# Opening of an attention and expert kernel: two projections moved in among the first score maxima, a row load moved behind the first unit's loads, fewer filler products

## The reference, cut to what matters

```python
# x: (8, 256, 512)   ctx: (8, 256, 512)   mask: (8, 1, 512)
x = x + xattn(layernorm(x), ctx, mask, mask, Wq, bq, Wk, bk, Wv, bv)
x = x + ffn(layernorm(x), router, shared experts, 8 routed experts, top 2)

def xattn(target, source, target_mask, source_mask, ...):      # 16 heads of 16
    q = Wq @ target + bq;  k = Wk @ source + bk;  v = Wv @ source + bv
    dot = einsum('bhdt,bhds->bhts', q, k) / 4
    mask = target_mask[..., None] * source_mask[..., None, :]
    amap = softmax(mask * dot - (1 - mask) * 1e6) * mask
    return einsum('bhts,bhds->bhdt', amap, v)
```

## Time and profile before

| | |
|---|---|
| Time before, median of 3 runs | 689.02 us (688.03 to 693.57) |
| Span of the profiled execution, first to last instruction | 651.7 us |
| Own time of the profiled execution | not shown beside its span |
| Busy share: PE, DVE, ACT, POOL | 93%, 78%, 72%, 55% |
| Chain that ended last, by engine | PE 76%, DVE 11%, issue 6%, ACT 5% |
| Stretch that the change touches | about 21 to 60 us of the span |

### The profile page before, as it was taken

One profiled execution on the slowest core, in us unless ns is written; L12 is line 12 of the kernel. 1 busy time (PEld: TensorE's weight loads), 2 busy tenths in 40 slices (PEclk: granted clock), 3 DMA queues, 4 the chain that ended last, 5 costly groups with the idle time before them and its releaser, 6 DMA issues.

```text
span 651.7 us, 12576 instructions
## 1 busy us (share of the span) xinstructions
PE 606.6 (93%) x4110; PEld 259.2 (40%) x4110; DVE 507.6 (78%) x970; ACT 472.0 (72%) x662; POOL 360.0 (55%) x494
## 2 busy tenths in 40 slices
PE   4799999999999999999999999879999999999987
PEld 4543333333333333333333332224554466666532
DVE  2479899999999999999999999964528654454577
ACT  3654899899899899899898888985432276667511
POOL 5559453684684684684684462251553577777310
PEclk9899999999999999999999999999999999999999
DMA  8642434534525535534433432115698533333178
GB/s 293 195 135 76 114 93 145 168 110 144 170 87 168 167 89 171 167 112 146 135 111 102 132 111 80 50 52 121 170 220 184 110 105 106 100 106 107 50 230 310
DMA packets 64990, 88.66 MB, mean 136 GB/s; under 512 B 12624, under 2 KB 45264, under 8 KB 63904
## 3 DMA queue, kind: packets, MB, share of 16 engines
q1 hardware_dynamic: 60032, 68.72, 34.4%
q0 software_dynamic: 4896, 19.14, 12.1%
HBM read 63.75 MB, written 32.74 MB: 148 GB/s over the span
## 4 chain that ended last, share of the span: by engine, by line
PE 76%; DVE 11%; issue 6%; ACT 5%; DMA 1%; POOL 1%; SPq 0%; ACTq 0%; DVEq 0%; POOLq 0%
PE PS L1083 17%; PE PS L986 11%; PE PS L1311 9%; PE PS L1055 8%; PE PS L1774 7%; DVE MX L996 7%; PE PS L845 5%; PE PS L1837 4%; PE PS L1585 4%; ACT E L1069 2%; PE PS L840 2%; PE PS L991 1%; PE PS L933 1%; PE PS L1732 1%; PE PS L929 1%
## 5 line engine op out<-in xcount | busy, mean ns | idle before, releaser
L996 DVE TENSOR_REDUCE MX<-PS 128x1 f32<-128x512 f32 x512 | 323.1, 683 | 17.3 <-PE PS L986 15.4
L1069 ACT ACTIVATE E<-PS 128x1024 f32<-128x1024 f32 x256 | 253.5, 1020 | 32.7 <-PE PS L1055 28.6
L986 PE MATMUL PS<-BIG 53*128 53x512 f16 x512 | 128.6, 384 | 12.2 <-DVE MX L996 10.8
L1083 PE MATMUL PS<-E,BIG 128*32 128x512 f32 x1024 | 136.4, 605 | 2.0 <-ACT E L1069 2.0
L1055 PE MATMUL PS<-BIG 55*128 55x512 f16 x512 | 101.2, 381 | 8.2 <-ACT E L1069 3.5
L879 POOL TENSOR_TENSOR ML<-BIG,ML 128x512 f32<-128x512 f32 x30 | 38.3, 1277 | 102.8 <-ACT BIG L855 102.6
L986 PEld LDWEIGHTS PS<-BIG 53*128 53x128 f16 x512 | 34.3, 93 | 134.0 <-DVE MX L996 120.1
L1796 DVE SCALAR_TENSOR_TENSOR E<-WP,PS 128x352 bf16<-128x352 f32 x39 | 20.3, 521 | 47.0 <-ACT WP L1786 47.0
L1774 PE MATMUL PS<-BIG,CT 128*128 x312 | 53.0, 313 | 1.8 <-DVE WP L1346 1.0
L855 ACT ACTIVATE BIG<-PS,BIG 128x256 f32<-128x256 f32 x64 | 35.7, 560 | 25.9 <-PE PS L840 14.5
L1856 POOL DMA_INDIRECT scr_ys<-SW,bvB x39 | 38.3, 981 | 20.8 <-DVE SW L1849 12.5
(11 more groups left out here) (261 smaller groups left out, 904.0 us busy)
## 6 DMA issues: line engine op xcount, KB each, us to landing
scr_parts<-WP SPq DMA_DIRECT2D x96, 128.0 KB
BIG<-scr_parts SPq DMA_DIRECT2D x64, 192.0 KB
BIG<-in_we POOLq DMA_DIRECT2D x8, 1088.0 KB, 14.1
scr_u<-ML SPq DMA_DIRECT2D x32, 256.0 KB, 3.0
X<-in_x SPq DMA_DIRECT2D x8, 512.0 KB, 6.5
CT<-in_ctx SPq DMA_DIRECT2D x8, 512.0 KB, 4.1
ML<-scr_u SPq DMA_DIRECT2D x16, 256.0 KB
ML<-scr_recs SPq DMA_DIRECT2D x16, 256.0 KB
```

Of the source, the lines that this page charges most:

```text
L986: e.matmul(PS[:, yi[name] % 3, :], QK[rows, qb(u), 0, j0 + jj, 128 * tt:128 * tt + 128], QK[rows, qb(u), 1, j0 + jj, :], start=True, stop= ...
L996: e.tensor_reduce(MX[:, g % 2, c:c + 1], PS[:, yi[name] % 3, :], AX.X, ALU.max)\
L1069: e.activation(E[:, st, 2 * jj:2 * jj + 2, :], PS[:, slot(name):slot(name) + 2, :], ACT.Exp, scale=1 / 1024).then_inc(s["rc"], 1)
L1083: ins = e.matmul(PS[32 * hh:32 * hh + 32, AVB, :], VT[:, b % 2, st, 4 * (g % 4) + hh, :], E[:, st, hh, :], start=(st == 0), stop=(st == 3))
```

## The change

- `WARM` goes from (3, 1) to (1, 1): one filler product instead of three behind each score product of group 0.
- The two halves of k of unit 1 move from in front of the score products of group 0 to behind the fourth and the eighth of them. The two parts of v of unit 1 move from the same place to behind the tenth and the twelfth.
- With them move what is placed relative to them: the splitting of k on POOL, the writes of k, the scaling of v, and the load of source and mask of batch 2 on SP, which now stands behind the read-back of q of unit 1 instead of in front of it.
- The load of x of batch 2 moves on SP from in front of the writes of k of unit 0 to behind the read-backs of q and k of unit 0.
- ACT's scaling of the shared weights (`upper`) moves from -.95 to -.8, behind the two copies of k. POOL's `lower` moves from -.9 to -.7, behind the splitting of k, and so in front of the scaling of v of unit 1.
- The read-back of k of unit 1 moves a little later, to stand behind its writes.

```diff
-WARM = (3, 1)
+WARM = (1, 1)
...
         for w in range(NU):
+            tk = (-.93, -.82) if w == 1 else (w - 3 + 6.65 * IT, w - 3 + 7.85 * IT)
             ring += [(w - 3 + 3.75 * IT, ("q", w, 0)), (w - 3 + 4.75 * IT, ("q", w, 1)),
-                     (w - 3 + 6.65 * IT, ("k", w, 0)), (w - 3 + 7.85 * IT, ("k", w, 1))]
-            tv = -1 - .25 * IT if w == 1 else w - 2 + 0.65 * IT
+                     (tk[0], ("k", w, 0)), (tk[1], ("k", w, 1))]
+            tv = -.72 if w == 1 else w - 2 + 0.65 * IT
             mring += [(tv, ("v", w, 0)), (tv + (.1 if w == 1 else 1.0499999999999998) * IT, ("v", w, 1))]
...
         for b in range(2, B):
-            sp.at(2 * b - 6 + .02, load_x(b))
+            sp.at(-1.5 if b == 2 else 2 * b - 6 + .02, load_x(b))
...
-            act.at(-.95, upper)
+            act.at(-.8, upper)
...
-                pool.at(-.9, f)
+                pool.at(-.7, f)
...
-            sp.at(w - 2 + (2.9 if i else .9) * IT if w else -1.8 + .05 * i, emit)
+            sp.at(w - 2 + (3.6 if i and w == 1 else 2.9 if i else .9) * IT if w else -1.8 + .05 * i, emit)
```

## The result

The changed kernel takes 705.94 us (median of 5, 704.75 to 711.96) where the kernel before takes 689.02 (688.03 to 693.57): ratio 1.0257, 95% interval 1.0209 to 1.0304. It is 16.9 us slower; the forecast was 0.8 us faster. When it was measured again in another session (a session is one set of measurements, the kernel before among them) it took 673.94 beside 656.83, ratio 1.0262 (1.0226 to 1.0298), 17.1 us. The stage of the experts, which the change does not touch, took some 35 us more in the first two sessions than in the last two, for every kernel alike, so each kernel is compared only with the kernel before of its own session. Three executions of one experiment and five of another, whose mean clock was low, are left out of their ratios, but they are told of there, since whether the clock holds is the question.

What follows compares the result with a forecast made beforehand. It took PE's own work to bound 27.4 to 47 us. Terms: -3.2 (start of group 0) + 0.0 (group 0) + 2.3 (half clock) + 0.1 = -0.8, so 689.0 becomes 688.2 us; range 685.3 to 692.0.

Steps and rivals of the forecast that it cites:

- How long it lasts: PE from the start of group 0: half clock lasts 5.1 us, bounds 3.8 and 6.9.
- term of 2.3 us in the sum: PE in group 0: loss from half clock, 5.1 us at 0.455 us each, bounds 1.7 to 3.1.
- The first rival: PE from 28.7 us: half clock stays; 696.1 if through all of group 0, 690.9 if some 11 us; chance 0.16.
- The rival's price for group 0, 10.2 us: Group 0 wholly at half clock: 16 x 0.96 + 4 x 1.71 = 22.2 us, 10.2 more; a quarter of 0.16.
- What I held against it: Against lasting half clock: PE never idle (0.96 against DVE's 0.62), halves of k as dense as work that raised it.
- Fillers for real work, group 0 at 12.0 us at full clock: PE in group 0: 32 fillers (3.5 us) replaced by four projections (3.4 us), so it stays at 12.0 us.
- Start of group 0: First score product at 31.8 us instead of 35.03, after k's read-back: 3.2 us won, bounds 1.5 to 3.5.
- my signs of being wrong: First score product after 33.5, clock back after 39, PE waiting for `place` near 58 or 72, or group 2's shift lost.
- Row load: Load of x of batch 2 on SP: issued at about 30, 0.49 us, in front of nothing that is due.
- ACT, POOL and SP: Work moved off PE's path hides with 1 to 3 us to spare; 0.1 us charged, bounds 0 and 0.9.
- The 37.3 us between median and span: Whole kernel: the median is 37.3 us above the profiled span of 651.7, and the change has no hold on that.
- Everything behind group 1 shifts as a whole: From group 1 on, the order of work is the same and shifts as a whole, by -0.8 us in sum.

Runs made afterwards that it cites:

- the run with the gap closed: Changed kernel with 28 fillers ahead of the sum of squares of batch 1 and 56 ahead of the first score product: 655.03 us beside 656.98, ratio 0.9975.
- the run with the row load alone: Kernel before with only the load of x of batch 2 moved behind the read-backs of unit 0: 693.35 us, ratio 0.9989.
- the filled gap with 36 fillers: Changed kernel with 28 fillers ahead of the sum of squares, 36 ahead of the first score product: 692.49 us, ratio 0.9971 (eight of eleven executions).
- warm projections in front: Kernel before with the load of x of batch 2 moved and 28 fillers ahead of the sum of squares: 663.1 us, ratio 0.9999 (better five).
- the dense run: Changed kernel with 30 fillers ahead of the first score product, none ahead of the sum of squares: 656.16 us, ratio 1.0000.

## Why the prediction was wrong

The step that failed is "How long it lasts", 5.1 us with bounds of 3.8 and 6.9. It lasted 42 us, from 34.77 to about 77, and 48 us in the second profile of the changed kernel. The term of 2.3 us in the sum measured 17.5 over both groups. I took the length from rises behind unbroken projections and carried it over to a stream of score products with fillers. The first rival had the mechanism and its sign, and was given 0.16. What I held against it was that PE would never be idle at half clock. That was right (busy 2.00 of every 2.00 us) and worth nothing: here the busy share did not tell whether the clock would rise. I also held against it that the two halves of k are as dense as the work under which the clock rose before. Each is, but it lasts 1.7 us and stands between score products; of the runs that came to group 0 at half clock with one filler, only the one with all four projections in one block of 5.9 us (37.65 to 43.58) had a rise in group 0, 4.8 us into it. The rival's price for group 0, 10.2 us, measured 8.6 (20.53 less 11.96), since a score product at half clock takes 0.86 us, not 0.96 (doubling the streamed part alone, my 0.85, had been right); but I let it end with group 0, and group 1, with one filler as well, paid 8.9 more. I had read from group 1 of the kernel before that one filler is enough "once the clock is up". The run with the gap closed bears that out, where projections stand in between; that it is not enough to bring it up is another question, which the profile of before could not answer, since it shows no score product at half clock.

The Trainium skill's warnings pointed the right way. The Trainium skill (TensorE: Matmul & The Clock Gate, section "HAM oscillation — how this bites in real kernels") warns of idle gaps, after which work starts at half clock, and its section "A second HAM failure mode: psum-queue depth-cycling" warns of streams that idle briefly between groups. The trace agrees with the first (half clock behind 3.2 and 4.2 us idle). The second goes only part of the way: in the kernel before with one filler the clock fell in a filler at 39.57 before PE had idled at all in that group, and in the changed kernel it stayed at half with PE never idle.

Point by point:
- Fillers for real work, group 0 at 12.0 us at full clock: right. In the run with the gap closed, group 0 went from 36.29 to 48.21, 11.9 us.
- Start of group 0: 3.2 us sooner was too much. Measured from the sum of squares, which itself moves by up to 3 us between profiles (26.4 to 29.4), the first score product came 7.6 us after it before (27.39 to 35.03), and 5.4 and 6.0 us in the two profiles of the changed kernel: 1.7 to 2.2 us won. The writes of k took 4.7 us (25.37 to 30.07), less than my 5.3, but from the issue of the read-back to the first score product it was 4.7 us, not 3.2. I had taken the end of the DMA traffic for the landing; besides, the load of x now goes out at 31.52, ahead of the landing, and may have slowed it. No run separates the two. Of my signs of being wrong, the first score product later than 33.5 (34.77) and the clock back later than 39 both came.
- Row load: hides, as said (0.9989 alone).
- ACT, POOL and SP: nobody waited for them in the opening. `place` went out at 67.02, with no stall behind it on PE that the profile shows.
- The 37.3 us between median and span, which I took for something around the program: wrong. The span of every run is 1.7 to 2.1 us under its time. The profile of before must be of a session in which the expert stage was shorter: from the first product of the shared expert to the end it has 201.8 us, the run with the row load alone 240.9.
- Everything behind group 1 shifts as a whole: right in the main, 16.8 us at the shared expert and 16.9 in the result, though in the second profile some of the loss fell into group 2.
- The 0.3% by which runs differ: too little. The first executions of the kernel before alone span 0.8% (688.03 to 693.57).

What stays open: why the filled gap with 36 fillers lost the clock in three executions of eleven and warm projections in front in six of ten, while 1.06 us idle behind the dense run did no harm in ten; why three fillers needed 7.8 us in group 0 and 21 in group 1; and why half clock ended soon after the start of group 2 in some profiles and 7 us later in others.

## What to carry to other kernels

Products that look like waste may be what holds PE's clock. Before taking them out, or before moving dense work from in front of a thin stage to behind a wait, look in the profile for the granted clock at the start of that stage and ask what would bring it back if it fell; a fully busy PE is no answer. Look as well at what the engine did in the stretch in which the clock rose, and whether the new order still has such a stretch. Where PE must wait for a DMA ahead of a thin stage, fill the wait with products up to the landing: 30 of them were worth 17.8 us here, and filling both waits, with the projections left in front, made the kernel 0.5% faster than it had been.

## What was not expected of the hardware

- A stream in which PE is busy all the time, half of its instructions score products over 53 rows with one filler of 256 columns each, with single projections in between, stayed at half clock for 42 to 48 us in the two profiles of the changed kernel, and stayed at full clock through both groups where it had begun so without a pause.
- The expert stage took some 35 us more in two of four sessions, in every kernel. The chain of waits of the run with the row load alone, of such a session, shows a part of it:

```profile
523.13 8.78 another core or an unknown queue
```

Eleven such pieces add up to 29.9 us there, but in the profile of the changed kernel of the first session, whose expert stage was as long, to under 8 us. PE idled in that wait, and the granted clock fell to half as well (0.75 in 528 to 532 us, 0.50 in 532 to 536). What this queue is, and what made the stage longer, no run here tells.
